# Four engines of a two-layer kernel in a new order: VectorE's two-operand work, GpSimd's scaling and copies, and the side and segment products

## The chip, the cores and the metric

One core of a Trainium2 chip runs one program. The time is that of the device for one execution, in microseconds (us); several executions are timed and their median is used. Beside them one execution is recorded by the hardware profiler, and every stretch, wait and duration below is read from that one.

## The reference

The program computes four blocks on 2048 rows of 128 numbers, each on the layer norm of its input and added to it:

```
x = x + attn(ln(x))     # 16 heads of 64; softmax over a masked row; @ w_o
x = x + ffn(ln(x))      # fp4 blocks of 16: quantise x, gate, up, h; down
x = x + mixer(ln(x))    # q k v a g; scan in chunks of 64; out_proj; silu MLP
x = x + tokenmix(ln(x)) # r, k of x and the row before; relu^2; W_v

# the mask of attn: own segment of 64, or a distance that 4 divides, up to 256
seg = pos // 64; local = seg[None, :] == seg[:, None]
dil = (diff > 0) & (diff % 4 == 0) & (diff <= 256)
allowed = local | dil
```

Everything is float32; only the order of the engines' work is at issue here.

## The kernel before, in words

The attention is cut into 32 windows: a pair of heads `p` (8 of them) and a quarter `w` of the rows (512 of them). A window has two parts that are joined in the softmax: the "band" (rows of one residue class modulo 4, 128 queries against 192 keys, four classes, two heads) and the "segment" (own 64 rows). The stages of a window are spread over the steps `t` of a loop written out by hand for each engine (`for t in range(FIRST_STEP, DRAIN)`, t = 6 to 32), with a head before it and a tail behind it in which the calls stand one by one. Each call waits on semaphores for what it reads, so a call that waits holds everything behind it on its engine.

TensorE (PE), in step t: `project(t, 1)` (keys, lines 403 to 405), `weigh(t-6, 0)` and `(t-6, 1)` (probabilities by values of the band, line 484), `turn(t-6, 3)` (transposes of the segment, line 464), `output(t-7)` (line 510), `turn(t-5, 0)`, `weigh(t-6, 2)` (the side keys, line 495), `scores(t-2, 0)` (line 422), `weigh(t-6, 3)` (segment, line 498), `scores(t-2, 1)`, `project(t, 0)` (queries), `turn(t-5, 1)`, `turn(t-5, 2)`. `scores(G, 0)` waits for `queries_by_class(G)` and `keys_by_class(G+1)`; `turn(U, 0)` for `scale_band(U, 0)`, and `turn(U, 3)` for `scale_seg(U)`; both `turn(U, 2)` and the next window's `turn(U+1, 0)` need the even transposing bank, which VectorE's `even_turned` empties.

ScalarE (ACT): `take_queries`, `take_keys`, `take_out` (copies out of PSUM), `odd_turned` (likewise), `band_exps` (line 569), `seg_exps` (line 577), `exp_difference` (line 616), and in the head `take_values` of even number (line 644).

VectorE (DVE): `band_max` (line 719), `seg_max` (lines 731 and 733), `seg_sums` (line 741), `differences` (lines 750 and 754), `factors` (lines 761 to 771), `even_turned` (line 780), `accumulate` (line 792), `quantise` (in steps 12 to 26, one of five parts a step), and in the head `take_values` of odd number (line 836).

GpSimd (POOL): `scale_band` (four instructions of line 948), `scale_seg` (line 957), `keys_by_class` (line 930), `queries_by_class` (line 938). The scaling needs `fac`, which `factors` makes.

SyncE (SP) issues all DMAs in an order of its own. For every window it sends the maxima and sums out to memory (`send_statistics`, once `band_exps` and `seg_sums` are done) and fetches them back in the other layout (`fetch_statistics`, line 314); `differences(F)` on VectorE waits for the landing. Between the two it stores values (line 268) and loads them by class.

The second half (`tokenwise`) handles the rows in four groups of 512. Its calls have short names, with the group in brackets: `x1`, `bn0`, `ag0`, `rs0`, `z0` are the residual and the layer norm, `qx0` to `qx8` and `xq` the fp4 rounding of the normalised rows, `gu` the gate and up products, `hm` gate times up, `qa..`/`qb..` with `hqa`/`hqb` the rounding of that product in two halves, `rs3` and the like small GpSimd statistics. GpSimd divides (`qx4`, `qa4`, `qb4`, line 1827) and scales back (line 1832); VectorE rounds in between (`..7` line 1564, `..8` line 1569), part of it with both operands in SBUF. `clear()` (lines 1520 and 1521) fills two tiles that are read much later.

What is said of a place in the program goes by these calls. A group's numbers in the table STEPS only count semaphores; they follow the order.

## Time and profile before

| | us |
|---|---|
| median of 3 executions | 473.04 |
| lowest and highest of them | 469.19 and 474.06 |
| span of the profiled execution, first to last instruction | 468.8 |
| lowest time less the profiled span | 0.4 |
| PE / DVE / ACT / POOL busy in the span | 444.4 / 394.0 / 333.3 / 296.6 |

A time of its own for the profiled execution is not given, only its span. It lies 0.4 below the lowest of the three and 4.2 below their median, so executions of this very program differ by about 1% among themselves. Busy time of the PE includes the pipeline of each product, and so overstates how full it is; the idle time and what ended it is the more reliable reading.

### The profile page before, as it was taken

How to read it: one execution, taken by the hardware profiler on the slowest of the kernel's cores; microseconds unless marked ns; L12 is line 12 of the kernel's file. 1: busy time of each engine (PE TensorE's matmuls, PEld its weight loads, DVE VectorE, ACT ScalarE, POOL GpSimd, SP SyncE). 2: the span in 40 equal slices, each digit the busy share in tenths (PEclk: the TensorE clock that was granted, in tenths of full speed). 3: DMA queues.
4: the chain of work that ended last, by engine and by line, in shares of the span. 5: the costliest groups of instructions: out<-in, count | busy, mean ns of one | idle time of the engine just before them, and what ended most of it. 6: DMA issues, size and time to landing. Idle time of an engine off the chain costs nothing.

```text
span 468.8 us, 17264 instructions
## 1 busy us (share of the span) xinstructions
PE 444.4 (95%) x6440; PEld 350.0 (75%) x6440; DVE 394.0 (84%) x1344; ACT 333.3 (71%) x975; POOL 296.6 (63%) x491
## 2 busy tenths in 40 slices
PE   7997899999999999999999999998987989999996
PEld 6685688888888888788887778887744757558775
DVE  6885798987888899889887698995899989998775
ACT  3686768868877877886786678695566579987533
POOL 4321488677666858667865588564669897674322
PEclk9999899999999999999999999999999999999999
DMA  7577852346335445344455565364000000000003
GB/s 224 183 246 209 247 142 52 73 99 133 80 74 112 76 79 105 76 85 94 98 108 124 112 124 108 75 125 91 1 1 0 0 2 1 1 0 2 1 0 91
DMA packets 136099, 40.53 MB, mean 86 GB/s; under 512 B 104977, under 2 KB 131025, under 8 KB 136017
## 3 DMA queue, kind: packets, MB, share of 16 engines
q1 hardware_dynamic: 135440, 38.38, 35.7%
q8 instruction: 52, 0.85, 0.8%
q10 hardware_dynamic: 576, 1.05, 0.6%
q14 instruction: 31, 0.25, 0.2%
HBM read 29.44 MB, written 9.96 MB: 84 GB/s over the span
## 4 chain that ended last, share of the span: by engine, by line
PE 59%; POOL 9%; DMA 8%; DVE 8%; ACT 7%; SPq 4%; issue 3%; ACTq 0%; POOLq 0%; DVEq 0%
PE psum L422 10%; PE psum L464 10%; PE psum L484 5%; PE psum L1186 5%; DMA w_rows_dram<-st 4%; PE psum L498 4%; PE psum L495 4%; PE psum L403 4%; PE psum L510 4%; PE psum L1181 3%; PE psum L405 3%; PE psum L404 3%; DMA st<-w_rows_dram 2%; POOL area L1827 2%; ACT pband L569 2%
## 5 line engine op out<-in xcount | busy, mean ns | idle before, releaser
L948 POOL TENSOR_SCALAR pband<-pband,fac 128x192 f32<-128x192 f32 x256 | 103.9, 424 | 80.6 <-DVE fac L771 80.4
L569 ACT ACTIVATE pband<-pband,st 128x192 f32<-128x192 f32 x256 | 113.1, 447 | 1.0 <-DVE st L719 1.0
L719 DVE CUSTOM_DVE_ANT_0 pband<-psum,band_mask 128x192 f32<-128x192 f32 x256 | 76.1, 353 | 0.1
L422 PE MATMUL psum<-keys,q_class 64*64 64x192 f32 (+2 forms) x1536 | 66.2, 274 | 0.0
L464 PEld LDWEIGHTS psum<-ident,pband 128*128 128x128 f32 x384 | 45.4, 141 | 21.4 <-issue 13.3
L422 PEld LDWEIGHTS psum<-keys,q_class 64*64 64x64 f32 x1536 | 57.6, 133 | 1.4 <-issue 1.4
L464 PE MATMUL psum<-ident,pband 128*128 128x128 f32 x384 | 53.0, 273 | 2.2 <-DVE pt L780 2.2
L569 ACT ACTIVATION_READ_ACCUMULATOR pband<-pband,st 128x1 f32 x256 | 49.3, 192 | 0.0
L938 POOL COPY q_class<-q_rows 128x512 f32<-128x512 f32 x32 | 36.5, 1142 | 19.2 <-ACT q_rows L609 19.2
L930 POOL COPY keys<-k_rows 128x512 f32<-128x512 f32 x32 | 36.1, 1130 | 14.0 <-ACT k_rows L601 7.1
L780 DVE COPY pt<-psum 128x512 f32<-128x512 f32 x64 | 43.7, 683 | 0.5
L585 ACT COPY pt<-psum 128x512 f32<-128x512 f32 x64 | 37.1, 580 | 4.6 <-PE psum L464 4.5
L741 DVE TENSOR_REDUCE st<-pseg 128x8 f32<-128x512 f32 x32 | 21.9, 685 | 21.5 <-ACT pseg L577 21.3
L609 ACT COPY q_rows<-psum 128x512 f32<-128x512 f32 x32 | 18.7, 585 | 28.1 <-PE psum L405 28.0
L498 PE MATMUL psum<-pt,v_seg 64*64 64x64 f32 x1024 | 35.5, 218 | 1.1 <-issue 1.1
L1181 PE MATMUL psum<-xt,arena 128*128 128x512 f32 x72 | 35.1, 603 | 0.8 <-ACT xt L1422 0.8
L403 PE MATMUL psum<-xn_hi,w_hi 128*128 128x512 f32 x64 | 31.1, 486 | 4.7 <-ACT q_rows L609 4.0
L957 POOL TENSOR_TENSOR pseg<-pseg,fac 128x512 f32<-128x512 f32 x32 | 33.8, 1055 | 2.8 <-DVE fac L771 2.8
L484 PEld LDWEIGHTS psum<-pt,v_both 128*64 128x64 f32 x512 | 27.3, 136 | 10.5 <-issue 10.5
L484 PE MATMUL psum<-pt,v_both 128*64 128x128 f32 x512 | 35.0, 279 | 0.0
L498 PEld LDWEIGHTS psum<-pt,v_seg 64*64 64x64 f32 x1024 | 32.7, 135 | 1.3 <-issue 1.3
L510 PE MATMUL psum<-o_sb,wo 128*128 128x512 f32 x64 | 33.0, 597 | 0.1
(213 smaller groups left out, 1090.7 us busy)
## 6 DMA issues: line engine op xcount, KB each, us to landing
v_rows_dram<-arena SPq DMA_DIRECT2D x32, 256.0 KB, 3.4
v_both<-v_rows_dram SPq DMA_DIRECT2D x32, 256.0 KB, 3.8
v_seg<-v_rows_dram SPq DMA_DIRECT2D x64, 128.0 KB, 3.6
v_side<-v_rows_dram SPq DMA_DIRECT2D x96, 64.0 KB, 2.6
w_rows_dram<-st SPq DMA_DIRECT2D x64, 8.0 KB, 3.0
st<-w_rows_dram SPq DMA_DIRECT2D x64, 8.0 KB, 2.5
arena<-_attn_hidden_states_dram SPq DMA_DIRECT2D x4, 256.0 KB, 3.7
out_dram<-x SPq DMA_DIRECT2D x4, 256.0 KB, 2.5
```

The costliest lines, as they stand in the source:

```text
L403: pe.matmul(shared_bank[:, :], hi, xn_hi[:, cols], start=True, stop=False)
L422: return pe.matmul(bank[2 * r + head][rows, at:at + y.shape[1]], x, y, start=True, stop=True, skip_group_check=True)
L464: last = pe.transpose(turn_bank[odd][:, P * k:P * (k + 1)], src, ident[:, :])
L484: last = pe.matmul(by_class[dims, c, :], v_both[:, c, w, dims], turned[:, P * k:P * (k + 1)], start=(b == 0 and k < 2), stop=False, skip_g ...
L498: last = pe.matmul(out_bank[dims, cols], v_seg[dims, 2 * (TW * w + k) + half, :], turned[dims, cols], start=False, stop=(k == 3 and half = ...
L510: pe.matmul(shared_bank[:, :], wo[:, U // NW, :], o_sb[:, :], start=True, stop=True).then_inc(s_mix, 1)
L569: act.activation(x, x, ACT.Exp, bias=mine[:, head:head + 1], scale=-1.0, accum_out=mine[:, 2 + head:3 + head]).then_inc(s_exp, 1)
L585: act.copy(pt[:, PT_SLOTS + e % PT_SLOTS, :], turn_bank[1][:, :]).then_inc(s_pt[1], 1)
L719: dve.tensor_tensor_reduce(pband[:, G % P_SLOTS, c, head, :], bank[2 * r + head][:, at:at + BAND], band_mask[:, (0, 1, 1, 2)[w], SEG * (1 ...
L780: dve.tensor_copy(pt[:, e % PT_SLOTS, :], turn_bank[0][:, :]).then_inc(s_pt[0], 1)
L948: pool.tensor_scalar(x, x, fac[:, F % 2, 1, c, head:head + 1], 1.0, ALU.mult, ALU.mult).then_inc(s_scaled, 1)
L1181: end(pe.matmul(bk(g, to)[:, :], w, x, start=True, stop=True, skip_group_check=True), g, "tensor")
```

## The change

Nothing is computed differently and no instruction goes or comes: the calls of four engines stand in another order, in the head, in the loop and in the tail. SyncE's order is the same. In the loop:

```diff
 TensorE
                 turn(t - 5, 0)
+                scores(t - 2, 0)
                 weigh(t - 6, 2)
-                scores(t - 2, 0)
                 weigh(t - 6, 3)
...
 ScalarE
                 band_exps(t - 2, 0)
+                seg_exps(t - 2)
                 odd_turned(t - 5, 3)
-                seg_exps(t - 2)
                 band_exps(t - 2, 1)
...
 VectorE
-                differences(t - 4)
-                even_turned(t - 5, 0)
...
                     quantise((t - QUANT_STEP) // 5, (t - QUANT_STEP) % 5)
+                differences(t - 4)
+                even_turned(t - 5, 0)
                 factors(t - 4)
                 band_max(t - 2, 0)
+                even_turned(t - 5, 2)
                 seg_max(t - 2, 0)
-                even_turned(t - 5, 2)
                 seg_max(t - 2, 1)
                 band_max(t - 2, 1)
+                accumulate(t - 6)
                 seg_sums(t - 2)
-                accumulate(t - 6)
...
 GpSimd
                 scale_band(t - 5, 1)
-                keys_by_class(t)
-                scale_seg(t - 5)
-                scale_band(t - 4, 0)
                 queries_by_class(t - 1)
...
+                scale_seg(t - 5)
+                scale_band(t - 4, 0)
+                keys_by_class(t)
```

In the head, TensorE's `project(3, 0)` is followed before by `values(22); values(23); values(24); project(5, 1); values(25)` and now by `values(24); values(23); project(5, 1); values(26); values(25)`. ScalarE's `exp_difference(0)` stood before `take_queries(3)` and now stands behind it, behind `take_values(24)` and `take_keys(5)`; VectorE's `take_values(23)` still stands behind `differences(0)`, now with `seg_max(2, 1)` between them, and `seg_sums(2)` has moved from before `take_values(23)` to behind `take_values(29)`.

In the tail the calls of `tokenwise` change places with their neighbours:

```diff
 VectorE
-            ... seg_sums(31); differences(30); clear(); even_turned(29, 0) ... even_turned(29, 2)
-            differences(31); qx0(0); qx1(0); qx2(0); even_turned(30, 0); factors(31); accumulate(29)
-            even_turned(30, 2); qx7(0); qx8(0); x1(1); xq(0); bn0(1); ag0(1)
+            ... seg_sums(31); differences(30); even_turned(29, 0) ... even_turned(29, 2); even_turned(30, 0); qx0(0)
+            differences(31); qx1(0); qx2(0); factors(31); accumulate(29); even_turned(30, 2); qx7(0); x1(1); bn0(1)
+            ag0(1); qx8(0); xq(0)
 GpSimd
-            qx4(3); qa1(1); qb4(0); xq(3); qa4(1); hqa(0); hqb(0); qa1(2); qb1(1); qb4(1); qa4(2); hqa(1)
+            qx4(3); qb4(0); qa1(1); xq(3); hqa(0); qa4(1); hqb(0); qb1(1); qa1(2); qb4(1); hqa(1); qa4(2)
```

In these rows, taken from the programs, a line's number is that of its own program. First GpSimd's step in the loop, before: the first half of one window's band is scaled (`pband`), then come the queries, the other half, the keys and the segment (`pseg`).

```order
L948 TENSOR_SCALAR pband<-pband,fac 128x192 x4
L938 COPY q_class<-q_rows 128x512
L948 TENSOR_SCALAR pband<-pband,fac 128x192 x4
L930 COPY keys<-k_rows 128x4x128
L957 TENSOR_TENSOR pseg<-pseg,fac 128x512
```

And now, from the same scaling on:

```order
L943 TENSOR_SCALAR pband<-pband,fac 128x192 x4
L925 COPY keys<-k_rows 128x4x128
L943 TENSOR_SCALAR pband<-pband,fac 128x192 x4
L933 COPY q_class<-q_rows 128x512
L952 TENSOR_TENSOR pseg<-pseg,fac 128x512
```

The two copies have changed places: the keys now follow directly on the scaling that has to wait for `fac`.

TensorE's part of a step with a middle quarter before, from `turn(t-5, 0)` on, with the side products (`v_side`) ahead of the first scores (the scores have six rows more of products like the two shown, cut away in both):

```order
L464 MATMUL psum<-ident,pband 128x128 x4
L495 MATMUL psum<-pt,v_side 64x64 x16
L422 MATMUL psum<-keys,q_class 64x192 x2
L422 MATMUL psum<-keys,q_class 64x128 x2
...
L422 MATMUL psum<-k_rows,q_rows 64x64 x8
L498 MATMUL psum<-pt,v_seg 64x64 x16
```

And now:

```order
L464 MATMUL psum<-ident,pband 128x128 x4
L422 MATMUL psum<-keys,q_class 64x192 x2
L422 MATMUL psum<-keys,q_class 64x128 x2
...
L422 MATMUL psum<-k_rows,q_rows 64x64 x8
L495 MATMUL psum<-pt,v_side 64x64 x16
L498 MATMUL psum<-pt,v_seg 64x64 x16
```

The scores have moved ahead of the side products, which now touch the segment products; all of it is the same 64x64 work.

VectorE at the end of the attention before, from `differences(30)` on (`joint`, `diff`), with the number behind a name for the group:

```order
L754 TENSOR_TENSOR diff<-joint,st 128x32
L1520 MEMSET mark 128x512
L1521 MEMSET zt0 128x1
L780 COPY pt<-psum 128x512
...
L1564 SCALAR_TENSOR_TENSOR area0<-psum,area0 128x512
L1569 SCALAR_TENSOR_TENSOR area0<-psum,area0 128x512
L1526 TENSOR_TENSOR arena<-arena,psum 128x512
L1744 TENSOR_TENSOR z0<-area0,sc0 128x512
L1530 BN_STATS st1<-arena 128x6 x4
L1535 BN_AGGR mv1<-st1 128x2 x4
```

And now:

```order
L750 TENSOR_TENSOR diff<-joint,st 128x32
L776 COPY pt<-psum 128x512
...
L1559 SCALAR_TENSOR_TENSOR area0<-psum,area0 128x512
L1521 TENSOR_TENSOR arena<-arena,psum 128x512
L1525 BN_STATS st1<-arena 128x6 x4
L1530 BN_AGGR mv1<-st1 128x2 x4
L1564 SCALAR_TENSOR_TENSOR area0<-psum,area0 128x512
L1739 TENSOR_TENSOR z0<-area0,sc0 128x512
```

The memset of `mark` has left the place behind `diff` (it stands 39 rows further on), and group 1's statistics (`st1`, `mv1`) have moved ahead of `qx8(0)` and `xq(0)`.

## Rows read from the trace of the kernel before

**Rows 1.** The page, busy time, share and instructions of each engine.
```profile
PE 444.4 (95%) x6440; PEld 350.0 (75%) x6440; DVE 394.0 (84%) x1344; ACT 333.3 (71%) x975; POOL 296.6 (63%) x491
```

**Rows 2.** Stretches (start:end, length): busy time and instructions of each engine, clock, DMA share, GB/s.
```profile
40.00:50.00 10.00, 5.96 (x22) 4.05 (x21) 4.98 (x23) 5.04 (x18) 1.60 (x2) 0.89 0.92 269
...
62.00:220.00 158.00, 158.00 (x3128) 131.12 (x3128) 138.25 (x546) 123.13 (x407) 113.83 (x202) 1.00 0.45 90
222.00:271.00 49.00, 47.07 (x899) 38.41 (x899) 38.30 (x152) 35.26 (x118) 31.86 (x56) 1.00 0.53 114
...
320.00:345.00 25.00, 23.40 (x315) 18.36 (x313) 20.21 (x60) 14.80 (x30) 16.89 (x34) 1.00 0.16 35
345.00:386.00 41.00, 35.19 (x173) 23.43 (x174) 38.18 (x83) 26.69 (x52) 36.14 (x42) 1.00 0.00 1
386.00:420.00 34.00, 32.48 (x176) 21.44 (x175) 31.54 (x63) 31.39 (x72) 24.79 (x35) 1.00 0.00 1
420.00:464.70 44.70, 44.62 (x279) 34.00 (x277) 34.91 (x93) 23.56 (x58) 15.44 (x19) 1.00 0.02 5
```

**Rows 3.** The chain in order of time, `output` of five windows: start, length.
```profile
116.20 0.86 PE psum L510 x2
...
125.46 0.86 PE psum L510 x2
...
134.25 0.86 PE psum L510 x2
...
215.29 0.86 PE psum L510 x2
...
272.36 0.86 PE psum L510 x2
```

**Rows 4.** Who waited for whom: us in total, times, longest.
```profile
POOL pband L948 <- DVE fac L771: 80.4, 30, 5.7
...
DVE st L741 <- ACT pseg L577: 21.3, 25, 1.6
...
DVE joint L750 <- DMA st<-w_rows_dram: 13.3, 6, 4.8
...
PE psum L403 <- ACT q_rows L609: 4.0, 1, 4.0
```

**Rows 5.** Timeline of one step of the loop: start, length.
```profile
207.37 1.14 POOL L930 COPY keys<-k_rows 128x512 f32<-128x512 f32 x1
...
212.39 1.62 POOL L948 TENSOR_SCALAR pband<-pband,fac 128x192 f32<-128x192 f32 x4 [2.87 <-DVE fac L771]
...
216.51 0.97 PE L495 MATMUL psum<-pt,v_side 64*64 64x64 f32 x26
217.27 0.38 PE L422 MATMUL psum<-keys,q_class 64*64 64x192 f32 x2
```

**Rows 6.** Groups of instructions by line: busy, mean ns of one, idle before.
```profile
L731 DVE TENSOR_REDUCE st<-psum 128x4 f32<-128x256 f32 x64 | 26.8, 419 | 0.3 <-PE psum L422 0.3
...
L609 ACT COPY q_rows<-psum 128x512 f32<-128x512 f32 x32 | 18.7, 585 | 28.1 <-PE psum L405 28.0
```

**Rows 7.** Timeline of the way out of the attention.
```profile
318.54 0.48 DVE L1520 MEMSET mark<- 128x512 f32 x1
...
319.79 1.06 PE L464 MATMUL psum<-ident,pband 128*128 128x128 f32 x8 [1.38 <-DVE pt L780]
...
331.96 0.69 DVE L1569 SCALAR_TENSOR_TENSOR area<-psum,area 128x512 f32<-128x512 f32 x1
...
335.28 0.19 POOL L1873 TENSOR_SCALAR rs<-mv 128x4 f32<-128x4 f32 x1 [0.39 <-DVE mv L1535]
```

**Rows 8.** The tail: durations (min/median/max ns) of one line, and its timeline.
```profile
L1827 POOL TENSOR_TENSOR area<-area,iv x8: 1382/1387/2038, 350.7 to 383.3; 128x704 f32<-128x704 f32 x8
...
358.32 1.05 DVE L1569 SCALAR_TENSOR_TENSOR area<-area 128x704 f32<-128x704 f32 x1
...
364.73 3.90 POOL L1827 TENSOR_TENSOR area<-area,iv 128x704 f32<-128x704 f32 x2 [0.55 <-DVE iv L1559]
...
383.38 2.20 DVE L1737 TENSOR_SCALAR hb<-arena,mv,rs 128x128 f32<-128x128 f32 x4 [0.92 <-POOL rs L1877]
```

More of the change, by code:

```diff
@@ L557, in _ @@
-            pr(2); t6(1); fc2(3); k(0); pr(3); r(0); t6(2); k(1); k(2); kv(0); t6(3); r(1); kv(1); r(2); k(3); kv(2)
-            r(3); kv(3)
+            weigh(27, 0); weigh(27, 1); turn(27, 3); output(26); turn(28, 0); weigh(27, 2); scores(31, 0)
+            weigh(27, 3); scores(31, 1); weigh(28, 0); turn(28, 1); output(27); turn(28, 2); turn(28, 3)
+            weigh(28, 1); weigh(28, 2); weigh(28, 3); turn_weights(0); turn(29, 0); output(28); turn(29, 1)
+            turn_weights(1); turn_weights(2); t1(0); turn(29, 3); turn_weights(3); turn_weights(4); turn_weights(5)
@@ new lines, in _ @@
+            turn(29, 2); weigh(29, 0); weigh(29, 1); turn(30, 0); weigh(29, 2); weigh(29, 3); turn(30, 1)
+            turn_weights(6); turn_weights(7); output(29); turn(30, 2); weigh(30, 0); weigh(30, 1); turn(30, 3); t1(1)
+            weigh(30, 2); weigh(30, 3); turn(31, 0); turn(31, 1); output(30); turn(31, 3); t2(0); turn(31, 2)
+            weigh(31, 0); gu0(0); t1(2); weigh(31, 1); weigh(31, 2); weigh(31, 3); gu1(0); output(31); t2(1); t1(3)
+            gu2(0); gu0(1); gu3(0); gu1(1); t2(2); gu2(1); gu0(2); gu1(2); t2(3); gu3(1); gu0(3); gu2(2); t3a(0)
@@ L560, in _ @@
+            fc1(3); fc0(3); k(0); t6(1); fc3(3); fc2(3); t6(2); k(1); pr(3); k(2); r(0); r(2); r(1); kv(0); t6(3)
+            kv(1); k(3); kv(2); r(3); kv(3)
         @block.scalar
@@ L901, in _ @@
              xr, k1, k2, o0, o) = tail_vector(dve)
-            differences(29); band_max(31, 0); factors(29); even_turned(28, 0); seg_max(31, 0); seg_max(31, 1)
-            even_turned(28, 2); band_max(31, 1); accumulate(27); seg_sums(31); differences(30); clear()
-            even_turned(29, 0); accumulate(28); factors(30); x1(0); bn0(0); ag0(0); even_turned(29, 2)
-            differences(31); qx0(0); qx1(0); qx2(0); even_turned(30, 0); factors(31); accumulate(29)
-            even_turned(30, 2); qx7(0); qx8(0); x1(1); xq(0); bn0(1); ag0(1); even_turned(31, 0); xqt(0)
@@ L917, in _ @@
-            x23(1); x5(0); h2t(2); h2(3); bn4(0); x23(2); x5(1); ag4(0); bn4(1); x23(3); ag4(1); z3(0); z3(1); xr(0)
-            x5(2); zt_(1); bn4(2); ag4(2); xr0(1); k2(0); z3(2); x5(3); bn4(3); ag4(3); xr(1); k1(1); z3(3); xr(2)
-            xr0(3); o0(1); o0(0); xr(3); o0(2); o(2); o0(3); o(3)
+            even_turned(28, 0); differences(29); band_max(31, 0); factors(29); seg_max(31, 0); seg_max(31, 1)
+            even_turned(28, 2); band_max(31, 1); accumulate(27); seg_sums(31); differences(30); even_turned(29, 0)
@@ new lines, in _ @@
+            accumulate(28); factors(30); x1(0); bn0(0); ag0(0); even_turned(29, 2); even_turned(30, 0); qx0(0)
+            differences(31); qx1(0); qx2(0); factors(31); accumulate(29); even_turned(30, 2); qx7(0); x1(1); bn0(1)
+            ag0(1); qx8(0); xq(0); even_turned(31, 0); accumulate(30); xqt(0); even_turned(31, 2); qx0(1); qx2(1)
+            x1(2); hm0(0); bn0(2); ag0(2); qx7(1); qx8(1); clear(); hm1(0); accumulate(31); qa0(0); qx0(2); x1(3)
+            qx2(2); bn0(3); hm2(0); ag0(3); qa2(0); qx7(2); hm0(1); qx8(2); hm3(0); qb0(0); qx0(3); hm1(1); qx2(3)
@@ L921, in _ @@
+            o(3)
         @block.gpsimd
```

150 lines of the change are left out of this document (70 added, 80 removed).

## The prediction

> **What bounds the kernel now.** I read the shares first, then stretches, then the chain and the waits. The shares [rows 1] name TensorE: 95% busy, 24.4 of 468.8 us idle. An average over stages decides nothing, so the stretches come next [rows 2]. From 62 to 220 TensorE is never idle. Between 222 and 271 it loses 1.9 us. Between 345 and 386 it idles 5.8 of 41 us while VectorE is busy for 38.2 and GpSimd for 36.1: there those two set the pace. From 420 to 464.7 TensorE has work again all the time (44.62 of 44.70). The head has one hole, in the stretch 40 to 50, with TensorE busy for 5.96 of 10 us.
>
> Is the loop bound by TensorE's work or by something it waits for that busy time hides? The chain answers [rows 3]: from one `output` to the next it takes 9.26 us (125.46 less 116.20) in a step of a middle quarter and 8.79 (134.25 less 125.46) in a step of an edge quarter, which has 8 of 16 side products less. VectorE's work varies from step to step with the part of `quantise`, and the two periods do not follow it. So each step is as long as TensorE's own instructions, and an order that leaves these instructions alone can't shorten it. The other engines do wait a lot [rows 4]: GpSimd 80.4 us for `fac`, VectorE 21.3 us in `seg_sums` for the segment's exponentials. That is slack, not time.
>
> Time can therefore go, or come, in four places only: the hole in the head, the stretch 222 to 271, the way out of the attention, and the tail up to 420.
>
> **The change part by part.** No instruction is added or removed, so each part is priced by who waits afterwards.
>
> *The loop, TensorE.* In before the side products stand ahead of `scores(t-2, 0)`, now behind them. The sum of the products is the same, and all of them are 64x64 work before and after, so nothing is switched more or less often. That the two kinds of weighing touch is priced at 0. A bound from the row [rows 5]: the side products hold TensorE for 0.76 us (217.27 less 216.51) for 32 instructions, 0.024 us each. If two of them were saved or lost at the seam, that is 0.05 us a step, and 1.3 us over 27 steps, either way. I take 0.
>
> *The loop, VectorE and ScalarE.* `seg_sums` moves behind `accumulate`, so its wait (21.3 us in 25 waits, 0.85 each [rows 4]) is covered by the addition. This is VectorE's own idle time, and TensorE does not wait for it: worth 0 at the end, but `fac` comes about 0.8 us earlier in a step. `quantise` ahead of `differences` costs nothing either, as long as the even bank is empty when `turn(t-5, 2)` wants it.
>
> *The loop, GpSimd: the cover that gets thin.* In before the keys are copied at 207.37 and are ready at 208.5, and the scores that read them are the next step's, at 217.27 [rows 5]: 8.8 us of margin. Now the copy stands behind `scale_band(t-4, 0)`, which waits for `fac`: 212.39 + 1.62 + 1.14 = 215.15 by the same rows, about 0.8 less for the earlier `fac`. The scores would start at 216.51, since the side products no longer stand before them. So 1.4 to 2.2 us of margin remain, enough in a plain step: cost 0. What is queued behind a late copy is GpSimd's next band, and TensorE's scores.
>
> *222 to 271.* Six steps take 57.07 us (272.36 less 215.29 [rows 3]); four of 9.26 and two of 8.79 would be 54.6. The 2.5 us are lost where fetched statistics land late. SyncE's order sets that, which is untouched, and `differences` still stands before `even_turned(t-5, 0)`. Bounds: the whole 2.5 us gained, and, if all of VectorE's waits of this kind in the later stages (13.3 less 4.8 = 8.5 [rows 4]) fell on TensorE, 6.0 us lost. I take 0.
>
> *The head.* In before TensorE stops before `project(5, 1)`, because `take_queries(3)` stands on ScalarE behind `exp_difference(0)`, which waits for `differences(0)`, which waits for a landing: 4.0 us [rows 4]. Now ScalarE takes the queries first. TensorE gets two sets of three products further, and then stops before `values(25)`: its bank is emptied by `take_values(23)`, which is behind `differences(0)` on VectorE. A set costs 0.8 us (5.96 us for 22 products is 0.27 each [rows 2]; part of them ran at the lower clock, the granted 0.89 of this stretch, so this is an upper value, and 0.7 a fair one). So 1.4 us of work is done earlier. The stop ends later, though: before it ended one ScalarE copy (0.585 [rows 6]) behind the exponential; now VectorE does `seg_max(2, 1)` (two instructions of 0.42 each [rows 6]) and a copy of the same size, about 0.5 to 0.8 more in all. Gain 1.4 - 0.5 = 0.9 at best 1.6. `seg_sums(2)` has moved back behind `take_values(29)`, so the statistics of window 2 leave later, by some 2 us; the loop's first steps have to swallow that. Bounds: 4.0 gained, 2 lost. I take a gain of 0.9.
>
> *The way out of the attention.* `differences(30)`, then the memset of 0.48, then `even_turned(29, 0)`, for which TensorE idles 1.38 [rows 7]: with the memset gone, 0.5 us less. Then group 1's layer norm: GpSimd's `rs0(1)` at 335.28 waited 0.39 for VectorE's statistics, and these stood behind `qx8(0)` (0.69) and `xq(0)` (about as long). Now they stand ahead. GpSimd is then held by its own scaling of window 31, which starts earlier as `factors(31)` does. Together I take 1.5 us for the start of the stretch 345 to 386: the 0.5, and 1.0 of the 1.4 that the two operations took. Bounds: 0.5 and 2.5.
>
> *The tail.* Where VectorE reads two SBUF operands while GpSimd works, both are stretched. GpSimd's division takes 1.387 us alone, 2.04 beside the 1.05 us operation at 358.32, and 3.90 for two at 364.73, where 2.77 would do [rows 8]: 0.65 + 1.13 = 1.8 us on an engine that is nearly full there. `hqa(0)` now follows its VectorE operation and `qa4(1)` comes after, so some of these meetings go. But the meetings are made by both engines' timing, and shifted starts bring others. I take 0, with 3.8 gained and 3 lost as bounds. The first is the 1.8 and as much again for GpSimd's small statistics up to 420; the second is one more stretched division for each of four groups, at 0.65.
>
> The sum: 0.9 + 0 + 0 + 1.5 + 0 = 2.4 us less. The profiled span of 468.8 becomes 466.4. The span is 4.2 below the median of the three timings, and I leave that distance as it is: 473.0 - 2.4 = 470.6.
>
> The Trainium skill's page "GPSIMD Engine Reference" (section Specifications) says that GpSimd's SBUF interfaces are shared with VectorE, and that VectorE collides with it when it has two SBUF inputs, or runs in a two-port mode. The first half is what the division rows show. The second speaks against the change's rule: at 383.38 four VectorE operations with a single SBUF tensor took 2.20 us beside a GpSimd division [rows 8], and an order that moves two-operand work alone leaves those. By that rule less of the 1.8 us would go. I set the tail at 0 without it.
>
> **The rivals.** *A: the meetings do go.* The tail's GpSimd and VectorE stretch is the bound between 345 and 386 [rows 2], so every stretched operation there that lies on both is paid in full. Then 3.8 us come on top of the 2.4: 473.0 - 6.2 = 466.8. For it speaks that both engines are at 88% and 93% there. Against it: the diff swaps a few neighbours, and five of the eight divisions already ran at 1.39.
>
> *B: slower, by GpSimd's keys.* The mechanism is the thin margin above. From a landing that is later than 1.4 to 2.2 us after its usual place, `fac`, the scaling, the keys and then `scores` are late in one row, where before only `even_turned` was. The place is 222 to 271 and the first steps of the loop, after the later send of window 2. Price: all 8.5 us of the later waits for statistics reach TensorE rather than 2.5, +6.0, and the head's gain is gone, while 1.5 on the way out stay: 473.0 + 6.0 - 1.5 = 477.5. Against it: `even_turned` blocks TensorE at about the same lateness, so the keys mostly add nothing to a delay already paid.
>
> *C: TensorE's loop was not full.* If VectorE's round was the true period, the 21.3 us of waits in `seg_sums` [rows 4] come out of the loop: 473.0 - 21.3 = 451.7. The Trainium skill's page "Trainium Kernel Development and Optimization" (Performance Expectations) calls matmul busy time a bad metric, since matmuls are pipelined, and asks for the weight loads' share. By that rule TensorE has room: the loads are busy for 131 of 158 us. Against C stands that two step lengths repeat to 0.01 us whatever VectorE does.
>
> **How the numbers follow.** The forecast has 0.50, A 0.28, B 0.16, C 0.04, and 0.02 is left for a loss that I don't see. About 1% (4.7 us) is what a measurement of this kernel can tell from no change. Faster by more: of the forecast 0.09 (it is 2.4, give or take 2.5), of A 0.20, of C 0.04: 0.33. Slower by more: 0.13 of B, 0.01 of the forecast, and the 0.02: 0.16. The rest, 0.51, is within 1%. The likeliest time is 470.6; its own range is 467 to 474. The whole range reaches to A and 3.3 beyond it at one end (the meetings are worth at most 3.8, the way out up to 1.0 more and the head 3.1 more than taken), and to B at the other: 463.5 to 477.5.
>
> **What would show it.** In the changed kernel's chain, `output` to `output` must again take 9.26 and 8.79 us; other periods make the loop's zero wrong. TensorE's hole in the head must be ended by VectorE's copy of `values(23)`, with about 4 us, and the loop must start about 1 us earlier. GpSimd should wait less for `fac`, and none of TensorE's waits should be for `keys`; if one is, B holds. `rs0(1)` should start 1.5 us nearer to the end of the head than before. The divisions' mean should stay near the 1.6 us it has now; a mean of 1.4, with a tail shorter by more than 3 us, is A. I am wrong as a whole if the stretch 222 to 271 changes by more than 2.5 us, for then the statistics' round trip, which I took as given, is what the order moved.

## The result, and the profile after

The changed kernel takes 476.24 us (median of 6 executions, 474.86 to 478.60), the kernel before 471.56 (6 executions, 469.19 to 474.06). The ratio is 1.0113, with a 95% interval of 1.0074 to 1.0151: slower by 1.1%, where 0.5% faster was forecast. The profiled execution has a span of 475.1, 6.3 more than before's. In the runs that give both, an execution's time is 1.9 to 2.1 us above its span; by that before's profiled execution took about 470.8, an ordinary one, and the changed one 477.0.

The shares on the page tell nothing of this: TensorE is again busy for 95%.

```profile
PE 450.4 (95%) x6440; PEld 350.9 (74%) x6440; DVE 397.8 (84%) x1344; ACT 332.0 (70%) x975; POOL 295.2 (62%) x491
```

I read the chain next, at the places of [rows 3] (start, length).

```profile
76.70 0.86 PE psum L510 x2
85.98 0.86 PE psum L510 x2
...
112.87 0.86 PE psum L510 x2
122.14 0.86 PE psum L510 x2
...
212.63 0.86 PE psum L510 x2
221.43 0.86 PE psum L510 x2
278.10 0.86 PE psum L510 x2
```

The periods of the loop are what they were: 9.28 (85.98 less 76.70), 9.27 and 8.80. From 221.43 to 278.10 it takes 56.67, before 57.07. But the first `output`, which stood at 70.84 before, stands at 76.70. Nearly all of the 6.3 us is there before the first head is done. By the start of the 32 outputs I cut both programs into three: up to the first `output` 70.68 and 76.54, from it to the last one 271.98 and 271.28, from there to the end 126.1 and 127.3. So the head lost 5.9, loop and way out gained 0.7, and the part behind the last `output` lost 1.2.

The stretches show the head's loss at 66 to 77 as two things: no work for TensorE, and the lower clock after it (columns as in [rows 2]; at 0.72 of full speed more than half of the stretch ran at 1.2 GHz rather than 2.4). The low clock at 50 to 54 stands behind the stop before `values(25)` and is no loss against before, which ran at 0.57 from 48.4 to 51.7, behind its own stop.

```profile
50.00:54.00 4.00, 3.28 (x44) 2.70 (x45) 1.98 (x6) 4.00 (x15) 1.74 (x2) 0.72 0.87 255
66.00:71.00 5.00, 3.76 (x104) 3.27 (x95) 0.76 (x3) 1.99 (x9) 1.64 (x2) 1.00 0.44 107
71.00:77.00 6.00, 4.86 (x29) 3.35 (x30) 5.83 (x27) 4.60 (x15) 4.37 (x10) 0.72 0.47 115
...
351.00:392.00 41.00, 35.42 (x181) 24.02 (x180) 39.44 (x84) 26.25 (x52) 35.04 (x43) 1.00 0.00 1
```

The second of these rows is the one to stop at: in 5 us VectorE is busy for 0.76, ScalarE for 1.99 and GpSimd for 1.64. All four engines wait at once, so the cause is outside of them. The same two stretches of the kernel before:

```profile
66.00:71.00 5.00, 5.00 (x69) 4.01 (x60) 4.83 (x20) 3.57 (x12) 3.43 (x8) 1.00 0.50 121
71.00:77.00 6.00, 6.00 (x156) 5.18 (x155) 5.36 (x24) 4.70 (x18) 3.67 (x7) 1.00 0.16 11
```

The chain of the changed kernel leads through it. Here it is from 57.28 to 74.14 us.

```profile
57.28 0.69 DVE arena L832
57.97 0.60 DVE st L737
...
58.63 0.36 SPq L306
...
60.46 0.42 SPq L268
...
63.05 0.53 SPq L292
...
66.53 0.43 SPq L314
...
67.00 3.68 DMA st<-w_rows_dram
...
70.70 0.21 DVE joint L746
70.93 0.20 DVE diff L750
...
72.39 0.48 ACT q_rows L605
...
72.91 0.80 PE psum L403
73.71 0.43 PE psum L404
```

Read from the top: VectorE copies `values(29)` (L832), then does `seg_sums(2)` (L737). Only then can SyncE send the statistics of window 2 (L306, at 58.63). Behind that stand four stores of values (L268), the side loads (L292) and another store, and then the fetch (L314) at 66.53. It lands at 70.7, and `differences(2)` of the loop's first step begins (L746). `even_turned` stands behind it on VectorE, and TensorE's transposes wait for the bank. Before, these statistics left at 54.42, were fetched at 61.61, and `differences(2)` ran at 64.63 without a wait. The queue between the two takes 7.2 us before and 7.9 now, so the 4.2 us by which the send is late are handed through whole. The landing is later still, by 6.2 us (70.67 for 64.46): the second transfer of the fetch took 3.7 us from its issue where it took 2.4 before. TensorE came to this place 1.7 us later than before (`project(6, 0)` starts at 68.36 for 66.62), so of the 5.9 us of the head 1.7 had been lost ahead of the stop; 2.4 are idle time at it (2.11 and 0.27), and most of the rest is the slower products behind it.

The waits that answer to [rows 4], with two that are new:

```profile
POOL pband L943 <- DVE fac L767: 77.6, 28, 5.2
...
DVE joint L746 <- DMA st<-w_rows_dram: 16.4, 7, 4.2
...
DVE hb L1732 <- POOL rs L1872: 5.4, 4, 1.4
...
PE psum L464 <- DVE pt L776: 3.8, 2, 2.1
...
DVE st L737 <- ACT pseg L573: 0.9, 1, 0.9
```

VectorE's 21.3 us of waits in `seg_sums` are gone (0.9), as they should be, and the loop is not a hundredth faster for it: 14.1 us of new ones stand in front of `even_turned`, where VectorE waits for TensorE's transposes. TensorE never waits for `keys`. For [rows 8]: the median and the longest of GpSimd's eight divisions are within 0.02 us of what they were.

```profile
L1822 POOL TENSOR_TENSOR area<-area,iv x8: 1384/1386/2027, 356.1 to 388.4; 128x704 f32<-128x704 f32 x8
```

### The profile page after: what moved, and what is told of

Its sections match the earlier page's. It is cut to its first block, busy times and chain, and to the rows that moved or that the text cites. A ratio compares the mean times of both kernels' runs of the same rounds, so it can differ in the third digit from the quotient of the medians.

```text
span 475.1 us, 17264 instructions
## 1 busy us (share of the span) xinstructions
PE 450.4 (95%) x6440; PEld 350.9 (74%) x6440; DVE 397.8 (84%) x1344; ACT 332.0 (70%) x975; POOL 295.2 (62%) x491
## 4 chain that ended last, share of the span: by engine, by line
PE 60%; DVE 13%; DMA 9%; SPq 5%; ACT 4%; issue 4%; POOL 4%; ACTq 0%; DVEq 0%; POOLq 0%
PE psum L422 10%; PE psum L464 10%; PE psum L484 5%; PE psum L498 4%; PE psum L510 4%; DMA w_rows_dram<-st 4%; PE psum L1181 4%; PE psum L495 4%; PE psum L403 4%; DMA st<-w_rows_dram 3%; PE psum L1176 3%; PE psum L405 2%; PE psum L404 2%; SPq L292 2%; PE psum L1172 2%
## 5 line engine op out<-in xcount | busy, mean ns | idle before, releaser
L565 ACT ACTIVATE pband<-pband,st 128x192 f32<-128x192 f32 x256 | 113.4, 448 | 0.4 <-DVE st L715 0.3
L422 PE MATMUL psum<-keys,q_class 64*64 64x192 f32 (+2 forms) x1536 | 62.6, 278 | 0.0
L422 PEld LDWEIGHTS psum<-keys,q_class 64*64 64x64 f32 x1536 | 53.9, 134 | 6.3 <-issue 6.2
L776 DVE COPY pt<-psum 128x512 f32<-128x512 f32 x64 | 43.9, 686 | 14.3 <-PE psum L464 14.1
L484 PE MATMUL psum<-pt,v_both 128*64 128x128 f32 x512 | 36.0, 282 | 0.0
L1176 PE MATMUL psum<-xt,arena 128*128 128x512 f32 x72 | 35.1, 609 | 0.9 <-ACT xt L1417 0.8
L422 PE MATMUL psum<-k_rows,q_rows 64*64 64x64 f32 x1024 | 30.1, 222 | 0.0
```

Of the source, the lines that this page charges most:

```text
L422: return pe.matmul(bank[2 * r + head][rows, at:at + y.shape[1]], x, y, start=True, stop=True, skip_group_check=True)
L484: last = pe.matmul(by_class[dims, c, :], v_both[:, c, w, dims], turned[:, P * k:P * (k + 1)], start=(b == 0 and k < 2), stop=False, skip_g ...
L565: act.activation(x, x, ACT.Exp, bias=mine[:, head:head + 1], scale=-1.0, accum_out=mine[:, 2 + head:3 + head]).then_inc(s_exp, 1)
L776: dve.tensor_copy(pt[:, e % PT_SLOTS, :], turn_bank[0][:, :]).then_inc(s_pt[0], 1)
L1176: end(pe.matmul(bk(g, to)[:, :], w, x, start=True, stop=True, skip_group_check=True), g, "tensor")
```

## The experiments

In all of them the first, the middle and the last part are read as above: start of the first `output`, from there to the last one, and from there to the end. "Head" is what stands ahead of the loops, "tail" what stands behind them. All interval ratios are to the kernel before, timed in the same series; its median there was 470.1 to 470.4 for the runs e1 to e15. The first two rows are from the result above.

| run | median, us | ratio (95%) | first output | to the last | to the end |
|---|---|---|---|---|---|
| before | 471.56 | | 70.68 | 271.98 | 126.1 |
| changed | 476.24 | 1.0113 (1.0074 to 1.0151) | 76.54 | 271.28 | 127.3 |
| e1 head back | 469.71 | 0.9997 (0.9965 to 1.0029) | 69.06 | 271.26 | 127.3 |
| e2 loop alone | 470.63 | 1.0018 (0.9987 to 1.0049) | 72.09 | 271.19 | 126.1 |
| e3 tail alone | 470.47 | 0.9991 (0.9966 to 1.0017) | 70.23 | 269.58 | 127.4 |
| e4 sums early | 473.05 | 1.0061 (1.0037 to 1.0086) | 73.16 | 270.14 | 127.4 |
| e5 sums late | 475.16 | 1.0092 (1.0058 to 1.0126) | 75.42 | 271.17 | 126.1 |
| e6 front and sums | 471.00 | 1.0014 (0.9986 to 1.0043) | 71.90 | 271.43 | 126.9 |
| e7 queries first | 470.16 | 0.9989 (0.9962 to 1.0016) | 68.96 | 271.92 | 126.1 |
| e8 exit alone | 469.20 | 0.9982 (0.9955 to 1.0009) | 69.17 | 269.98 | 126.3 |
| e9 hqb back | 471.47 | 1.0032 (1.0004 to 1.0060) | 71.14 | 271.12 | 127.2 |
| e10 hqb early | 471.19 | 1.0000 (0.9969 to 1.0032) | 73.25 | 271.25 | 126.4 |
| e11 three parts | 467.88 | 0.9968 (0.9936 to 1.0001) | 70.53 | 274.51 | 125.1 |
| e12 changed, mended | 471.14 | 1.0017 (0.9992 to 1.0042) | 73.21 | 270.50 | 127.2 |
| e13 last stretch new | 473.06 | 1.0059 (1.0027 to 1.0092) | 71.01 | 272.42 | 127.7 |
| e14 last stretch old | 469.93 | 0.9989 (0.9964 to 1.0015) | 72.15 | 268.71 | 126.5 |
| e15 three parts again | 468.73 | 0.9967 (0.9941 to 0.9993) | 71.46 | 269.43 | 126.2 |

The last column repeats to 0.5 us wherever the order is the same, but for e11, whose last output came late by itself (e15 is the same kernel). The other two vary more from one execution to the next: with an unchanged head the first output lies between 69.1 and 73.3 us (nine executions, the one of before among them). Part of this goes with TensorE's clock: in the two earliest (e1 and e8, 69.06 and 69.17) it was granted in full for the 9.5 us behind the stop before `project(5, 1)`, in the other seven (70.2 to 73.3) it was at 0.70 to 0.85. So single profiles say where, and the ratios say how much.

**Which part of the program.** First I put parts of one kernel into the other, all four engines together.

e1: changed kernel, head as before.

```diff
 TensorE (and so on ScalarE, VectorE and GpSimd)
-            values(22); values(21); project(3, 0); values(24); values(23); project(5, 1); values(26) ...
+            values(20); values(21); project(3, 0); values(22); values(23); values(24); project(5, 1) ...
```

> The changed kernel with the head of all four engines as before; loop and tail stay changed. Theory H (the head lost the time): the first output is at 70.7 us again instead of 76.5, and the median falls from 476.2 to about 471, a ratio to before of 1.00. Rival L (the loop's new order is what makes its first steps stall; the head itself is only 1.7 late): the first output is at about 74, and the ratio is 1.005 to 1.01. Rival T (the tail costs time too, 1.1 us from the last output to the end in the profiles): ratio 1.002 to 1.004, and the stretch from the last output to the end is 127.3 rather than 126.1.

e2: kernel before, with the changed loop.

```diff
                 turn(t - 5, 0)
+                scores(t - 2, 0)
                 weigh(t - 6, 2)
-                scores(t - 2, 0)
 and likewise the loops of ScalarE, VectorE and GpSimd
```

> The kernel before with the loop of all four engines changed, head and tail as before. Theory H: ratio 1.00, first output at 70.7, steps of 9.26 and 8.79 us as before. Rival L: a stall in the first steps of the loop, 2 to 4 us, ratio 1.005 to 1.01. A third outcome would be a gain in the stretch 222 to 271, where the changed kernel made up 1.0 us and gave 0.9 back in the next step: up to 1 us faster, ratio 0.998.

e3: kernel before, with the changed tail.

```diff
-            ... differences(30); clear(); even_turned(29, 0) ... qx7(0); qx8(0); x1(1); xq(0); bn0(1); ag0(1)
+            ... differences(30); even_turned(29, 0) ... qx7(0); x1(1); bn0(1); ag0(1); qx8(0); xq(0)
 and likewise the other three engines
```

> The kernel before with what stands behind the loop changed on all four engines. Theory H: the way out gains 0.7 (output of window 31 earlier by that much), the rest gives back 1.1, so ratio 1.00, with the stretch from the last output to the end at about 127.3 rather than 126.1. Rival T (the tail loses on its own): ratio 1.003 or more. Rival A of the prediction (collisions of VectorE and GpSimd gone): ratio 0.99, and no division over 1.5 us.

With the head of before the loss is gone (0.9997). The loop alone and the tail alone are each within 0.5% of before. So the loss is in the head, and the other theories (L and T) fall. The tail's stretch behind the last output is 1.2 longer in e1 and e3, as T has it; the way out is 0.4 and 1.0 shorter there. That the head is enough by itself is shown by e5 below.

**Which call of the head.** e4: changed kernel, one call moved up.

```diff
-            ... factors(0); take_values(25); take_values(27); band_max(3, 0); take_values(29); seg_sums(2); ...
+            ... factors(0); seg_sums(2); take_values(25); take_values(27); band_max(3, 0); take_values(29); ...
```

> The changed kernel with one call moved: seg_sums(2) on VectorE stands right behind factors(0) rather than behind take_values(29). Theory H with the late statistics of window 2 as its mechanism: they are sent at about 55.3 rather than 58.6, landing before 68, the 2.4 us that TensorE idles in step 6 and the lower clock behind them are gone, the first output is at about 73, and the median is 3 to 3.5 lower, 473. Rival S (SyncE reaches the fetch at 66.5 because of the value stores and loads in its queue, whenever the statistics leave): nothing changes, 476.

e5: kernel before, with the same call moved down.

```diff
-            differences(0); seg_sums(2); take_values(23); ... take_values(29); differences(1); take_values(31)
+            differences(0); take_values(23); ... take_values(29); seg_sums(2); differences(1); take_values(31)
```

> The kernel before with one call moved: seg_sums(2) on VectorE stands behind take_values(29), where the changed kernel has it, rather than behind differences(0). Theory H (late statistics of window 2 stop TensorE in the loop's first step): they are sent at about 58 rather than 54, TensorE idles 2 us or more in step 6 before the transposes, the first output is at 73 to 74.5 rather than 69 to 72, and the ratio to before is 1.005 to 1.009. Rival S (what SyncE has queued sets the fetch in any case): ratio 1.00. Rival R (only together with the head that is 1.7 late): ratio below 1.003.

e6: e4, with the first part of the head as before too.

```diff
-            keep_busy(4); values(1); values(0); values(3); turn_rows(1); values(2); project(0, 1); values(4) ...
+            keep_busy(4); values(0); values(1); values(2); project(0, 1); turn_rows(1); values(3); project(1, 1) ...
-            moments(0); normalise(0); split_v(0); split_qk(0, 1); split_qk(0, 0); take_lo(0); moments(1) ...
+            moments(0); normalise(0); split_v(0); split_qk(0, 1); take_lo(0); split_qk(0, 0); moments(1) ...
 and likewise ScalarE up to band_exps(0, 0)
```

> The changed kernel with seg_sums(2) early as in e4_sums_early, and with the first part of the head (up to the first scores on TensorE, the first band_exps on ScalarE, the first band_max on VectorE) in the order of before. Theory H: the first scores start at 24.3 instead of 26.0, the first output is 1.7 earlier than in e4 (71.5), ratio 1.001 to 1.003 rather than 1.006. Rival D (in the head the value stores and loads on SyncE set the pace, so that an earlier start is lost again before the loop): first output at 73, ratio 1.006.

e5 is the strongest of the runs: one call of 0.68 us, moved by some 10 us on an engine that has time, makes the kernel slower by 0.9%, nearly the whole loss. Its timeline has the same hole at the same place. What follows the hole is another thing, though: in e5 the clock stays at 1.00 (0.63 in the changed kernel, from 72.91 to 76.54), and TensorE waits for the load of `wo` instead, which SyncE issues behind this fetch (71.08 for 65.12 before). So the late queue is paid for twice there. The first output, at 75.42, is later than the 73 to 74.5 expected.

```profile
70.32 0.19 DVE L750 TENSOR_REDUCE joint<-st 128x16 f32<-128x32 f32 x1 [4.40 <-DMA st<-w_rows_dram]
...
71.49 0.63 PE L464 MATMUL psum<-ident,pband 128*128 128x128 f32 x4 [2.28 <-DVE pt L780]
...
75.42 1.12 PE L510 MATMUL psum<-o_sb,wo 128*128 128x512 f32 x2 [0.83 <-DMA wo<-in_L_attn_w_o_dram]
```

Rival S is refuted by it: the fetch moved with the send (58.60 and 66.56). R is refuted too, since it needs no late head. In the other direction (e4) the send came at 56.71 rather than the 55.3 expected, and the wait of VectorE for the landing is 0.72 rather than 4.2; half of the loss goes. The send stands in SyncE's queue behind the fetch of window 1, and that one was 2.1 late too (55.16 for 53.03 before); the first output waits 0.77 for `wo`. The other half goes when the first part of the head is as before (e6, 1.0014; e12 below, 1.0017). In that part the first scores start at 25.96 in the changed kernel (26.49 in e4) and at 24.29 before, after the same work: `take_lo(0)` stands behind `split_qk(0, 0)`, and more sets of values stand ahead of the projections. How much this part is worth rests on the ratios alone. The first scores expected at 24.3 in e6 came at 25.54, and with the first part as before they lie between 24.1 and 25.7 in the other profiles; the intervals of e4 and e6 just overlap. The two causes don't add up, and this would be why: once the statistics land at 70.3 (e5) or 70.7 (changed), the landing sets the time, and an earlier TensorE would only have waited longer for it.

**The part that I had priced at a gain.** e7: kernel before, ScalarE takes the queries ahead of the exponential.

```diff
-            seg_exps(2); take_values(22); exp_difference(0); take_queries(3); take_values(24); band_exps(2, 0)
+            seg_exps(2); take_values(22); take_queries(3); take_values(24); exp_difference(0); band_exps(2, 0)
```

> The kernel before with only the part of the change that my prediction priced at a gain of 0.9: on ScalarE take_queries(3) and take_values(24) stand ahead of exp_difference(0). By the prediction: the hole of 4.0 (3.2 in other executions) before project(5, 1) is replaced by one of 2.3 to 2.6 that ends at the copy of values(23), and the first output comes 0.9 earlier than in a run of before, ratio 0.998. Rival M (as in the changed kernel, the time is lost again behind the hole): ratio 1.00, first output between 69 and 72. Rival W (the first output waits for the load of w_o, as it did for 0.4 us in e1_head_back): ratio 1.00 with a wait for that load.

The hole is 2.38 and ends at the copy of `values(23)`, as reasoned. In the other profiles with this order it is 2.2 to 4.3 us long, so it doesn't always get shorter. The first output, at 68.96, is as early as in e1 and e8, though the clock was at 0.83 behind the stop. The time is 0.9989 with an interval that holds both 0.998 and 1: a gain of this size is neither shown nor refuted.

**The way out, and the tail.** e8: kernel before, with the changed way out alone.

```diff
-            differences(30); clear(); even_turned(29, 0) ... qx8(0); x1(1); xq(0); bn0(1); ag0(1) ... qx8(1); hm1(0)
+            differences(30); even_turned(29, 0) ... x1(1); bn0(1); ag0(1); qx8(0); xq(0) ... qx8(1); clear(); hm1(0)
 with the other engines up to the last output as changed
```

> The kernel before with the changed order from the end of the loop to the last output alone (for VectorE up to qx8(1), with the memset behind it); head, loop and the later tail as before. Theory: the way out gains 0.7 to 1.0 (61.7 us before from output 23 to output 31, 60.7 to 61.1 in the runs with the changed tail) and from the last output to the end it takes 126.1 as before, since the loss of 1.2 there came from the order after the last output: ratio 0.997 to 0.999. Rival: the loss of 1.2 belongs to the changed way out (its statistics ahead of qx8(0) and xq(0)), and the stretch behind the last output takes 127.3: ratio 1.00.

It takes 60.8 us from output 23 to 31 (278.31 to 339.15) rather than 61.7 (280.98 to 342.66), and 126.3 behind it: the way out gains a little in this profile, and the loss behind it is not its doing. The gain isn't shown in the time (0.9982, and the interval holds 1), and the profiles overlap: the changed order takes 60.4 to 61.3 us from output 23 to 31 in ten of them and 63.8 in e11, the old one 61.6 to 62.1 in five and 60.5 in e2.

Then I looked for that loss of 1.2. In the changed tail `hqb(3)`, which reads two SBUF operands, runs beside GpSimd's scaling and takes 1.68 us; before it took 0.88. This is the timeline of e3:

```profile
384.74 1.39 POOL L1832 TENSOR_TENSOR area<-area,sc 128x704 f32<-128x704 f32 x1
385.21 1.68 DVE L1744 TENSOR_TENSOR area<-area,sc 128x704 f32<-128x704 f32 x1
```

It looked like the very collision that the change is about, and on the path. e9 (e3 with it moved back) and e10 (before with it moved):

```diff
 e9
-            qb8(3); hqb(3); w(0); a1(0); aa(0)
+            qb8(3); w(0); a1(0); hqb(3); aa(0)
 e10
-            qb8(3); w(0); a1(0); hqb(3); aa(0)
+            qb8(3); hqb(3); w(0); a1(0); aa(0)
```

> The kernel of e3_tail_alone (only what stands behind the loop is changed) with one call moved back: on VectorE hqb(3), a product of two SBUF operands, stands behind w(0) and a1(0) as before and not ahead of them. Theory K (ahead of them it holds group 0's chain, and is stretched to 1.68 us by GpSimd's scaling beside it): it takes 0.9 again, and from the last output to the end it takes 126.0 to 126.4 rather than 127.35; ratio to before 0.996 to 0.997 rather than 0.999. Rival P (the loss of 1.2 is in the new order of TensorE's last products): the stretch stays at 127.3.

> The kernel before with hqb(3) alone moved ahead of w(0) and a1(0). Theory K: the operation takes about 1.7 instead of 0.88 if GpSimd's scaling is beside it, and the stretch from the last output to the end grows from 126.1 by 0.9 to 1.7, ratio 1.002 to 1.004. Rival P: it stays at 126.1, since group 0 has slack before TensorE's next product.

The stretch stays at 127.2, but e9 doesn't test K: in it `hqb(3)` takes 0.88 again, and `w(0)` (L1732), which reads two SBUF operands as well, now stands beside the same scaling and takes 1.59 instead of 0.68. The stretching has moved by one operation, and what follows starts 0.1 earlier. (That e9's ratio is 0.4% above e3's is not explained by it; their first outputs are 0.9 apart.)

```profile
387.21 1.40 POOL L1832 TENSOR_TENSOR area<-area,sc 128x704 f32<-128x704 f32 x1
387.56 1.59 DVE L1732 SCALAR_TENSOR_TENSOR area<-area 128x512 f32<-128x512 f32 x1
389.42 0.88 DVE L1744 TENSOR_TENSOR area<-area,sc 128x704 f32<-128x704 f32 x1
```

e10 costs 0.3 there, and its operation isn't even stretched (0.89). So I cut the tail in two. e13 is before with only the last stretch changed, e14 the changed tail with only the last stretch as before.

```diff
 the last stretch, on GpSimd and TensorE
-            rs3(2); rs3(3); rs4(0); rs4(1); shift_weights(); rs4(2) ...
+            rs3(2); shift_weights(); rs4(0); rs3(3); rs4(1); rs4(2) ...
-            pr(1); fc0(2); fc1(2); t5(3); fc2(2); fc3(2); fc1(3); fc0(3); t6(0) ...
+            pr(1); fc0(2); fc1(2); fc2(2); fc3(2); t5(3); t6(0); pr(2); fc1(3) ...
```

> The kernel before with the changed order only in the last stretch: TensorE behind pr(1), ScalarE behind rq0(3), VectorE behind h2(2), GpSimd behind rs3(2). If the loss of 1.2 is made there, the stretch from the last output to the end takes 127.2 to 127.4 and ratio 1.002; if it is made in the group-wise part before it, 126.1 and ratio 1.000.

> The counterpart: what stands behind the loop is changed up to that cut, and the last stretch is as before. If the last stretch carries the loss: 126.1 to 126.3 from the last output to the end, and with the gain of the way out ratio 0.998. Otherwise 127.3 and ratio 1.000.

The last stretch carries it: 127.7 and 126.5. This is what refutes K: e14 has `hqb(3)` stretched to 1.66, and e13 has it at 0.88. At most 0.4 (126.5 for 126.1) is left for it. In the waits, what differs first is VectorE waiting for GpSimd's root of the layer norm (L1878 in e13 and e14, L1877 and L1872 in before and after). First e13, then e14:

```profile
DVE hb L1738 <- POOL rs L1878: 6.3, 5, 1.4
```

```profile
DVE hb L1738 <- POOL rs L1878: 0.4, 1, 0.4
```

It is 1.3 before and 5.4 in the changed kernel. `shift_weights`, moved ahead of `rs4(0)`, is not what holds GpSimd there: in e13 it is done at 431.2, and GpSimd then stands idle for 4.99 us until VectorE's statistics come. VectorE waits because `z3` now follows, in three of four groups directly, on `ag4`, with GpSimd's root between the two. What reaches TensorE shows in its weight loads (e13):

```profile
436.18 0.19 POOL L1874 TENSOR_SCALAR rs<-mv 128x4 f32<-128x4 f32 x1 [4.99 <-DVE mv L1536]
437.76 0.30 PEld L1182 LDWEIGHTS psum<-xt,arena 128*128 128x128 f32 x2 [0.74 <-ACT area L1477]
438.53 0.38 PEld L1182 LDWEIGHTS psum<-xt,arena 128*128 128x128 f32 x2 [0.48 <-ACT area L1477]
439.82 0.86 PEld L1178 LDWEIGHTS psum<-ident,hb 128*128 128x128 f32 x8 [0.91 <-DVE hb L1758]
```

The same three waits (0.74, 0.48, 0.90) stand in the changed kernel and in e3; in before and e14 no weight load of this stretch waits over 0.31 for a ScalarE copy. The first two are `fc2(2)` and `fc3(2)`, which now stand directly behind `fc0(2)` and `fc1(2)`, without `t5(3)` between them, and need the banks that ScalarE empties. The third is `t5(3)`, for VectorE's `h2(3)`, which now stands behind `z3(0)` and needs `rs3(3)`; on GpSimd that root stands now behind `rs4(0)` and its 4.99 us, and starts 4.3 us later after the last output than before (94.1 for 89.9). So TensorE's own new order (rival P of e9) is a candidate for the 1.2 us, and so is that of VectorE and GpSimd; none was tried alone, and the cause within the last stretch stays open. Nor is it clear why e13's ratio is 0.6% where its profile shows 1.6 us (0.3%); 0.3 is inside its interval.

**All together.** e11 and e15 are one kernel: before, with e7, e8 and one thing that neither kernel has.

```diff
 SyncE
-            fetch_statistics(2); load_sides(0, 3); load_wo(); send_statistics(3)
+            fetch_statistics(2); load_wo(); load_sides(0, 3); send_statistics(3)
```

> The kernel before with the changed way out (e8), with take_queries(3) and take_values(24) ahead of exp_difference(0) (e7), and, which neither kernel has, with the load of w_o on SyncE ahead of the side loads of window 3 instead of behind them. If the first output is bound by that load (waits of 0.4 to 0.8 us in e1, e4, e5 and e8), the wait is gone and the first output comes at 68 to 68.7 instead of 69.0 to 70.7; with the way out's 0.9 the ratio is 0.994 to 0.996. If the load isn't the bound, ratio 0.997 to 0.998.

> The kernel of e11_three_parts once more: the ratio was 0.9968 (0.9936 to 1.0001). If the three parts gain, it is again at 0.995 to 0.998 and the two together exclude 1; if e11 was chance, it is at 0.999 to 1.001.

e12 is the changed kernel with e6, e9 and this load.

> The changed kernel with its three losses taken back: seg_sums(2) early, the first part of the head as before (both as in e6), hqb(3) behind a1(0) (e9), and the load of w_o earlier (e11). Theory H with K: the ratio to before falls from 1.011 to 0.997 to 0.999, with 126.1 behind the last output. If the loop or the middle of the head has a loss of its own that the others cover, it stays at 1.001 or above.

The three parts beat both kernels: 0.9968 (0.9936 to 1.0001) and, in a second series, 0.9967 (0.9941 to 0.9993), so 1.5 us less than before. The second interval excludes 1 and the first just holds it. The wait for `wo` at the first output (0.55 in e8's profile, below) is gone in both. The first output, expected at 68 to 68.7, came at 70.53 and 71.46, within the spread of the others, so the load's own share is not shown, nor is that of the two other parts.

```profile
69.17 1.13 PE L510 MATMUL psum<-o_sb,wo 128*128 128x512 f32 x2 [0.55 <-DMA wo<-in_L_attn_w_o_dram]
```

The kernel of e12 comes to 1.0017 (0.9992 to 1.0042): with the head's two causes and `hqb(3)` taken back, 1.1 us of the last stretch remain (127.2 for 126.1). The 0.997 to 0.999 expected counted on K for these. Its first output, 73.21, is at the late end of the spread, with a clock of 0.71 behind its stop.

## Why the prediction was wrong

**The loop at 0: right.** 9.28 and 8.80 where 9.26 and 8.79 were forecast, and 1.0018 (0.9987 to 1.0049) for the loop alone. The scores ahead of the side products, the thin margin of the keys and the 21 us of `seg_sums` waits were all worth nothing. Rival C is refuted by the last: of these waits 20 us went from `seg_sums`, and the period stayed. The 14 us of new ones in front of `even_turned` say the same: VectorE has time to spare in a step.

**222 to 271 at 0: right.** From output 16 to 22 56.67 for 57.07. The last two of these steps take 18.5 to 21.2 us in executions with the very same loop order, so what is lost there is a matter of the execution.

**The head at a gain of 0.9: the step that failed.** It had three pieces. The hole before `project(5, 1)` would be replaced by one that ends at the copy of `values(23)`: that is so (2.30 in the profile, shorter than my 4 or so, and 2.2 to 4.3 in all profiles with this order). The next sentence was the error: "`seg_sums(2)` has moved back behind `take_values(29)`, so the statistics of window 2 leave later, by some 2 us; the loop's first steps have to swallow that." They left 4.2 later, since the copies that `seg_sums(2)` now stands behind wait for TensorE's products, which I had not followed. And I gave the delay no price, though all for it was in the trace of before: SyncE's queue between this send and its fetch took 7.2 us, the statistics landed at 64.46, and `differences(2)` ran at 64.63. So there was 0.2 of slack, and no room to swallow even the 2 us. What the runs showed in its place: in the changed kernel the landing is 6.2 late (4.2 of the send, 0.7 of the queue, 1.3 of a slower transfer), and VectorE itself comes 1.9 later to it, so VectorE waits 4.2; that this equals the lateness of the send is chance. TensorE waits 2.1, and behind it stands the lower clock, by which the way from `project(7, 1)` to the first output takes 3.63 us (72.91 to 76.54) rather than 2.41 (68.27 to 70.68). My bound of "2 lost" had neither the queue nor what follows a stop in it (the clock here, the load of `wo` in e5). With the statistics alone late the kernel is slower by 0.9% (e5), with them early again by 0.6% (e4). The first part of the head I did not price at all: 1.67 us at the first scores in these two profiles. I had listed only the changes around the hole.

**The way out at 1.5: too much; 0.9 in the profiles, and not shown in the time** (medians of 61.7 us from output 23 to 31 with the old order and 60.8 with the changed one, and e8 at 0.9982 with an interval that holds 1). GpSimd's `rs0(1)` did start earlier, 35.1 us after output 25 (339.17 less 304.06) rather than 37.0, but about half of that at most arrives at the last output.

**The tail at 0: right up to the last stretch, which lost 1.2.** Its rounding part is as long as before (44 us behind the last output VectorE is at the same point to 0.1 us), with two stretched divisions for three. Rival A did not come true: the mean of the eight is 1.53 for 1.61 (six of 1.39, one of 2.03, one of 1.90), so one meeting of three went, and nothing came of it. The loss is in another place than any that I had looked at, in the new order around the layer norm's roots and the `fc` products at the end. Some of my bounds were also added up wrongly, without bearing on this: twice 1.8 is 3.6 and not 3.8, four times 0.65 is 2.6 and not 3, and 1.0 and 3.1 beyond A are 4.1 and not 3.3.

**Rival B** had the right source ("after the later send of window 2") and one of the right places (the first steps of the loop), and the wrong path: no wait for `keys` exists. Its time is right by luck (4.5 us slower, measured 4.7): its 6.0 of loss were all later waits for statistics reaching TensorE, and what came was one late send in the head. What I wrote against it was in fact the mechanism: "`even_turned` blocks TensorE at about the same lateness". At 0.16 it was priced as if a late landing were an accident, when the diff itself made it late.

## What to carry to other kernels

When an order moves a call, follow what it releases to the end of its chain, above all through a queue that issues in order: here a 0.7 us sum released a send, 7 us of other DMAs stood between that send and its fetch, and all engines waited at the far side. Price a new stop of TensorE with what follows it, not with the stop alone: slower products in the changed kernel, a second late transfer of the same queue in e5. And take an engine's wait, or an operation that a neighbour stretches to double its length, as time only once the period or the end has moved with it: 20 us of the one kind were worth nothing here, and 0.8 of the other at most 0.4. When you move a stretched operation away, look whether the next one is stretched in its place.

## What I had not expected of the hardware

The length of a stop does not say by itself whether the clock falls. After a stop of 3.16 us in e1 and of 2.75 in e8 the next 10 us ran at the full clock; after 2.38 in e7 and 2.30 in the changed kernel it fell (0.85 and 0.97 in e7's two stretches, 0.72 at 50 to 54 in the changed one). Nor does the order say it: e13, with the head of e8 and a stop of 2.81, ran at 0.70 in the 9.7 us behind it, and e5 kept 1.00 behind its second stop of 2.28, where the changed kernel fell to 0.63 after 2.11. Why is not shown. First e8, then e7:

```profile
40.00:50.00 10.00, 7.25 (x41) 4.95 (x39) 6.20 (x27) 6.34 (x23) 1.99 (x2) 1.00 0.94 285
50.00:60.00 10.00, 10.00 (x132) 8.25 (x124) 8.41 (x26) 7.66 (x25) 7.68 (x15) 1.00 0.83 237
```

```profile
40.00:50.00 10.00, 7.62 (x26) 4.96 (x24) 5.89 (x26) 6.01 (x20) 1.38 (x2) 0.85 0.95 298
50.00:60.00 10.00, 10.00 (x125) 8.36 (x126) 7.52 (x24) 7.42 (x24) 7.18 (x13) 0.97 0.82 225
```

And TensorE's busy time hid the tail's loss: from the last output to the end it is idle for 12.7 us in before and in e3, while e3 takes 1.2 us more; it is "busy" for 113.4 and 114.6 us with the same products. The Trainium skill's page "Trainium Kernel Development and Optimization" (section Performance Expectations) warns of just this, since matmuls are pipelined; the tail agrees with it, by these 1.2 us. The same section calls the busy share of the weight loads a good metric for how close a kernel is to its roofline. Read as room in the loop (83%, rival C), that share misled here: the step's length is TensorE's own.
